# An attention and expert kernel: scores on 48 stacked rows in 64x64 tiles, and the step of a batch written out in eight slots

## The reference

```python
qkv = x @ w_qkv.T                       # 16 heads, D = 8
att = einsum('bhqd,bhkd->bhqk', q, k) / sqrt(8)
att = where((j <= i) & (j >= i - 127), att, -inf)   # window of 128
out = einsum('bhqk,bhkd->bhqd', softmax(att), v)
x = layernorm(x + out @ w_out.T)
logits = x @ router_w; p = softmax(logits); top 2 of 8
y = sum over the two of p_e * (gelu(x @ w_in[e] + b_in[e]) @ w_out[e] + b_out[e])
x = layernorm(x + y)
```

## Time and profile before

| what | value |
|---|---|
| median of 3 runs | 224.44 us (224.05 to 225.66) |
| the profiled execution's own time | 223.83 us |
| its span, first to last instruction | 221.8 us |
| PE busy | 203.4 us (92%) |
| DVE busy | 182.9 us (82%) |
| ACT busy | 116.7 us (53%) |
| POOL busy | 89.2 us (40%) |
| mean granted TensorE clock | 0.96 of full speed |

### The profile page before, as it was taken

One profiled execution on the slowest core, in us unless ns is written; L12 is line 12 of the kernel. 1 busy time (PEld: TensorE's weight loads), 2 busy tenths in 40 slices (PEclk: granted clock), 3 DMA queues, 4 the chain that ended last, 5 costly groups with the idle time before them and its releaser, 6 DMA issues.

```text
span 221.8 us, 5963 instructions
## 1 busy us (share of the span) xinstructions
PE 203.4 (92%) x1906; PEld 135.9 (61%) x1908; DVE 182.9 (82%) x522; ACT 116.7 (53%) x270; POOL 89.2 (40%) x166
## 2 busy tenths in 40 slices
PE   7786999989999999999999999989999899999960
PEld 4332446555565565565566566656688798989950
DVE  6664655789979989989989998977899888988883
ACT  2200106647557557557557566769445756374530
POOL 7230003375445635635635536478244211422103
PEclk9997559999999999999999999999999999999996
DMA  4947751542633533533533431000000001000011
GB/s 113 282 117 240 202 148 46 151 147 77 170 120 104 163 110 99 162 104 99 160 104 99 158 104 29 5 26 3 0 4 0 0 3 45 7 24 24 3 47 47
DMA packets 20391, 19.66 MB, mean 89 GB/s; under 512 B 1609, under 2 KB 17937, under 8 KB 20369
## 3 DMA queue, kind: packets, MB, share of 16 engines
q1 hardware_dynamic: 20180, 19.30, 29.4%
q10 hardware_dynamic: 189, 0.09, 0.1%
HBM read 13.94 MB, written 5.24 MB: 86 GB/s over the span
## 4 chain that ended last, share of the span: by engine, by line
PE 63%; DVE 17%; issue 7%; ACT 4%; DMA 4%; POOL 1%; SPq 1%; DVEq 1%; POOLq 0%; ACTq 0%
PE bank L1051 12%; PE bank L1043 9%; PE bank L960 7%; PE bank L977 5%; PE bank L992 4%; PE bank L955 3%; PE bank L942 3%; PE bank L945 3%; PE bank L926 3%; PE bank L1089 3%; DMA ks<-k_scratch 2%; DVE rest L671 2%; DVE neg_max L748 2%; PE bank L978 2%; DVE parts L676 2%
## 5 line engine op out<-in xcount | busy, mean ns | idle before, releaser
L474 ACT ACTIVATE probs<-bank 128x384 f32<-128x384 f32 x128 | 60.0, 496 | 34.7 <-PE bank L978 32.5
L432 POOL TENSOR_SCALAR_AFFINE_SELECT probs<-probs 128x1024 f32<-128x1024 f32 x32 | 35.7, 1116 | 67.8 <-ACT probs L474 67.8
L813 DVE SCALAR_TENSOR_TENSOR x_rows<-bank,gate_c,x_rows 128x128 f32<-128x128 f32 (+1 forms) x128 | 36.6, 343 | 5.3 <-PE bank L1051 4.2
L748 DVE TENSOR_REDUCE neg_max<-bank 128x2 f32<-128x384 f32 x64 | 33.5, 546 | 3.4 <-PE bank L960 3.1
L1051 PE MATMUL bank<-w_out_sb,hid 128*128 128x128 f32 x256 | 34.2, 277 | 1.0 <-DVE x_rows L813 1.0
L1051 PEld LDWEIGHTS bank<-w_out_sb,hid 128*128 128x128 f32 x256 | 32.6, 191 | 3.4 <-DVE x_rows L813 1.4
L574 ACT ACTIVATE hid<-bank,b_in_sb 128x512 f32<-128x512 f32 x32 | 21.9, 687 | 22.4 <-PE bank L1043 22.3
L977 PE MATMUL bank<-qs,ks 75*128 75x256 bf16 x128 | 33.4, 279 | 0.1
L743 DVE TENSOR_REDUCE neg_max<-bank 128x4 f32<-128x512 f32 x32 | 21.9, 685 | 8.8 <-PE bank L945 8.1
L978 PE MATMUL bank<-qs,ks 75*128 75x128 bf16 x128 | 26.9, 218 | 0.0
L436 POOL TENSOR_SCALAR_AFFINE_SELECT probs<-probs 128x512 f32<-128x512 f32 x32 | 24.2, 756 | 0.0
(11 more groups left out here) (117 smaller groups left out, 343.8 us busy)
## 6 DMA issues: line engine op xcount, KB each, us to landing
qs<-q_scratch SPq DMA_DIRECT2D x16, 288.0 KB
ks<-k_scratch SPq DMA_DIRECT2D x16, 288.0 KB
q_scratch<-parts SPq DMA_DIRECT2D x8, 192.0 KB, 2.1
k_scratch<-parts SPq DMA_DIRECT2D x8, 192.0 KB, 2.4
x_cols<-x_t SPq DMA_DIRECT2D x8, 128.0 KB, 2.6
x_rows<-x SPq DMA_DIRECT2D x8, 128.0 KB, 2.2
k_scratch<-parts SPq DMA_DIRECT2D x8, 128.0 KB, 2.3
out<-y_sb SPq DMA_DIRECT2D x8, 128.0 KB, 1.8
```

The source lines that it names most:

```text
L432: pool.affine_select(out=own, in_=own, compare_op=ALU.is_ge, fill=0.0, base=0, pattern=[[0, 2], [0, 4], [1, P]], channel_multiplier=-1).th ...
L474: nc.scalar.activation(probs[g][:, :, i, :], st_banks(spare)[k % len(st_banks(spare))][:, 0:3 * P].rearrange("p (k c) -> p k c", k=3), ACT ...
L748: nc.vector.tensor_reduce(neg_max[:, 1, 4 * g + 2 * u:4 * g + 2 * u + 2], score_bank[1 + u][:, 0:384].rearrange("p (h c) -> p h c", h=2), ...
L813: nc.vector.scalar_tensor_tensor(token_rows(c, n), y_bank[e % 4][:, n * E:(n + 1) * E], gate_of(c, n, e), token_rows(c, n), ALU.mult, ALU. ...
```

## The change

Only 6 of the 9 products of parts stay, so a head takes 48 rows. Two heads stand one above the other in the stacks, on partitions 0 to 47 and 64 to 111, and there are 8 pairs of heads a batch, each in one piece of a stack; four stack buffers take the place of two, and all a batch's rows come in one set of four transfers. In `scores` each matmul uses a tile of 64x64 of the array, so that four (two heads, two halves of the queries) stand side by side; for the first 128 queries each half now takes only the keys that it needs. The mask's matmuls are cut into the same tiles. `turned_scores` computes a pair of heads in two tiles of 64 rows by 128 columns, each into its own bank, and there is one such pair of banks in place of two alternating banks. One exponential takes both heads of a pair.

The split into parts changes hands: PE subtracts the top part inside the bank (`subtract_top`), ACT takes the middle part, DVE only the low one. The maxima are split in two operations a batch instead of eight.

The loop and the steps go. Every engine now walks 75 slots, eight for each batch: batch b's scores start in slot 8b (six of the eight slots have a job), its maxima are turned in 8b+8, its pairs of turned scores stand in slots 8b+11 to 8b+18, and its tail in 8b+22 to 8b+31; the projection for it stands in slot 8b-14. The first 11 slots have `keep_warm(2)` in place of turned scores. The loads of the later x columns (768 KB), the output weights and all rows of x are issued after the stacks of batches 0 and 1. The split of the expert weights and the choice for the first half of the tokens stand in slots 64 and 65 on DVE. The normed rows are written straight to their final tile, and POOL's copy of them goes. The last batch's transposed rows and logits move from chunk 0 of the experts into chunk 1, and the second half's choice stands later in chunk 1. The chunks are written out too.

```diff
-BLK = PARTS * D
-ROWS = PARTS * BLK
+PRODUCTS = ((0, 1), (0, 0), (0, 2), (1, 0), (1, 1), (2, 0))
+ROWS = len(PRODUCTS) * D
+KROWS = ROWS + PARTS
-KROWS = ROWS + PARTS
+PAIRS = H // 2
 QUADS = H // 4
...
-LOAD_WARM_UP = 7
-WARM_UP = 34
+LOAD_WARM_UP = 8
+WARM_UP = 44
...
+TWO_BF16_ONES = 1.0019378662109375
+STACKS = 4
+TURN_MAX, VALUES, S2, PV = 8, 12, 11, 15
+COPY_O, TURN_O, TURN_ATTN, PROJECT_OUT, TURN_X1, LOGITS = 22, 23, 25, 26, 30, 31
+PROJECT_QK = -14
+LAST_S1, LAST_S2 = 8 * B - 1, 8 * B - 1 + S2
+SCORE_JOBS = {0: (False, 0), 1: (True, 0), 2: (True, 2), 4: (False, 4), 5: (True, 4), 6: (True, 6)}
...
+                sp.wait_ge(part_top, b + 1)
+                copies(b, 0, 0)
+                copies(b, 1, 0)
+                sp.wait_ge(part_mid, b + 1)
+                copies(b, 0, 1)
+                copies(b, 1, 1)
+                sp.wait_ge(part_low, b + 1)
...
+            def stack(b):
+                sp.wait_ge(scratch_written[b % 2], 80 * (b // 2 + 1))
+                if b >= STACKS:
+                    sp.wait_ge(st_ready, PAIRS * (b - STACKS + 1))
+                for i, operand in enumerate((qs, ks)):
+                    for r in range(2):
+                        sp.dma_start(operand[b % STACKS][64 * r:64 * r + ROWS, :, :],
+                                     scratch[b % 2, i, :, r, :].rearrange("a (n t) -> a n t", n=PAIRS)).then_inc(stacked[b % STACKS], 16)
+            def stack_max(b):
+                sp.wait_ge(max_copied, b + 1)
+                for r in range(2):
+                    sp.dma_start(qs[b % STACKS][64 * r + ROWS:64 * r + KROWS, :, :],
+                                 max_t[r * PARTS * PAIRS:(r + 1) * PARTS * PAIRS, :]).then_inc(max_stacked[b % STACKS], 16)
...
+            write_parts(0)
+            sp.wait_ge(ones_ready, 1)
+            stack(0)
+            write_parts(1)
             sp.wait_ge(ones_ready, 2)
+            stack(1)
+            sp.dma_start(x_t_sb[:, 2 * T:B * T], x_t[:, 2 * T:B * T]).then_inc(x_t_loaded[2], 16)
+            sp.dma_start(wout_sb[:, :], wout_t).then_inc(out_w_loaded, 16)
+            sp.dma_start(router_sb[:, :], router_w).then_inc(moe_w_loaded, 16)
+            sp.dma_start(b_in_sb[:, :], b_in_t).then_inc(moe_w_loaded, 16)
+            sp.dma_start(x_sb[:, :, :], x.rearrange("(n p) e -> p n e", p=P)).then_inc(x_loaded, 16)
+            sp.wait_ge(ones_ready, STACKS)
+            for slot in range(LAST_S1 + 2):
+                b = batch_at(slot, TURN_MAX)
+                if b is not None:
+                    stack_max(b)
+                b = batch_at(slot, PROJECT_QK + 2)
+                if b is not None:
+                    write_parts(b)
+                b = batch_at(slot, PROJECT_QK + 3)
+                if b is not None:
+                    stack(b)
+                if slot == 9:
                     sp.dma_start(w_in_sb[:, :, :], w_in.rearrange("e d h -> d e h")).then_inc(moe_w_loaded, 16)
                     sp.dma_start(w_out_sb[:, :, :], w_out.rearrange("e h d -> h e d")).then_inc(moe_w_loaded, 16)
...
+            for slot in range(LAST_S2 + 2):
+                b = batch_at(slot, PROJECT_OUT + 1)
+                if b is not None:
+                    first_deviation(b)
+                n = quad_at(slot + PV - S2 - 2)
+                if n is not None:
+                    mask_probs(*n)
...
+            def exponentials(b, p):
+                g = p // 2
+                if p % 2 == 0 and b:
+                    act.wait_ge(pv_done, QUADS * (b - 1) + g + 1)
+                act.wait_ge(st_ready, PAIRS * b + p + 1)
+                two = slice(2 * (p % 2), 2 * (p % 2) + 2)
+                nc.scalar.activation(probs[g][:, :, two, :].rearrange("p k j c -> p j k c"),
+                                     st[:, :, 0:3 * P].rearrange("p j (k c) -> p j k c", k=3), ACT.Exp, scale=SCALE).then_inc(exp_done, 1)
...
+            def take_middle(b):
+                act.wait_ge(part_rest, b + 1)
+                nc.scalar.activation(parts[b % 2][:, 1, :, :], projection_bank(b)[:, :].rearrange("p (a t) -> p a t", a=2), ACT.Copy).then_inc(part_mid, 1)
...
+            for slot in range(LAST_S2 + 1):
+                n = pair_at(slot)
+                if n is not None:
+                    exponentials(*n)
+                for offset, piece in ((TURN_MAX, copy_max), (TURN_ATTN, copy_attention), (PROJECT_QK, take_top), (PROJECT_QK + 1, take_middle),
+                                      (VALUES, pad_v), (COPY_O, copy_output), (TURN_X1, copy_x1), (LOGITS, copy_logits)):
+                    b = batch_at(slot, offset)
+                    if b is not None:
+                        piece(b)
+                if slot == LAST_S1 + 2:
+                    route_exponentials(EARLY, 1)
...
+            def take_low(b):
+                p = parts[b % 2]
+                dve.wait_ge(part_mid, b + 1)
+                nc.vector.tensor_tensor(p[:, 2, :, :], projection_bank(b)[:, :].rearrange("p (a t) -> p a t", a=2), p[:, 1, :, :],
+                                        ALU.subtract).then_inc(part_low, 1)
...
+            def split_max(b):
+                part = max_parts[b % 2]
+                upper = upper_half(part[:, :, :, :, :])
+                dve.wait_ge(maxima, JOBS * (b + 1))
+                nc.vector.tensor_tensor(part[:, :, :, 1, :], part[:, :, :, 0, :], upper[:, :, :, 0, :], ALU.subtract).then_inc(max_rested, 1)
+                dve.wait_ge(max_rested, b + 1)
+                nc.vector.tensor_tensor(part[:, :, :, 2, :], part[:, :, :, 1, :], upper[:, :, :, 1, :], ALU.subtract).then_inc(max_split, 1)
...
+            for slot in range(LAST_S2 + 1):
+                b = batch_at(slot, TURN_O + 1)
+                if b is not None:
+                    normalise(b)
+                b = batch_at(slot, PROJECT_OUT + 1)
+                if b is not None:
+                    first_stats(b)
+                    first_moments(b)
+                b = batch_at(slot, TURN_X1 - 1)
+                if b is not None:
+                    first_norm(b)
+                n = jobs_at(slot)
+                if n is not None:
+                    take_maxima(*n)
+                b = batch_at(slot, TURN_MAX - 1)
+                if b is not None:
+                    split_max(b)
+                b = batch_at(slot, PROJECT_OUT)
+                if b is not None:
+                    first_residual(b)
+                b = batch_at(slot, PROJECT_QK + 1)
+                if b is not None:
+                    take_low(b)
+                b = batch_at(slot, TURN_X1 + 1)
+                if b is not None:
+                    split_x1(b)
+                if slot == LAST_S1 + 1:
+                    split_weights()
+                    route_shift(EARLY, B // 2 - 1)
+                if slot == LAST_S1 + 2:
+                    choose(EARLY, 1)
...
+            def subtract_top(b):
+                pe.wait_ge(part_top, b + 1)
+                mm(projection_bank(b)[:, :], minus_bf[:, :], parts[b % 2][:, 0, :, :], start=False, stop=True, skip_group_check=True).then_inc(part_rest, 1)
...
+            def scores(b, second, pair, job):
+                q, k = qs[b % STACKS], ks[b % STACKS]
+                heads, width = (2, 192) if second else (4, P)
+                if job % JOBS == 0:
+                    pe.wait_ge(stacked[b % STACKS], 64 * (b // STACKS + 1))
+                for r in range(2):
+                    if job + r >= 3:
+                        pe.wait_ge(maxima, job + r - 2)
+                    bank = score_bank[(job + r) % 3][:, 0:heads * width].rearrange("p (h c) -> p h c", h=heads)
+                    rows = slice(64 * r, 64 * r + 64)
...
+                        mm(at, ident_bf[rows, 64 * r:64 * r + 64], mask, start=True, stop=True)
+                for i in range(heads):
+                    for r in range(2):
+                        rows = slice(64 * r, 64 * r + ROWS)
+                        bank = score_bank[(job + r) % 3]
+                        for half in range(2):
+                            lo = 64 * half
+                            if second:
+                                keys, queries = slice(lo, lo + 192), slice(P + lo, P + lo + 64)
+                            else:
+                                keys, queries = slice(0, 64 + lo), slice(lo, lo + 64)
+                            last = mm(bank[lo:lo + 64, i * width:i * width + keys.stop - keys.start], q[rows, pair + i, queries], k[rows, pair + i, keys],
+                                      start=False, stop=True, skip_group_check=True)
+                        if i == heads - 1:
+                            last.then_inc(scores_ready, 1)
...
+            def turned_scores(b, p):
+                q, k = qs[b % STACKS], ks[b % STACKS]
+                if p == 0:
+                    pe.wait_ge(max_stacked[b % STACKS], 32 * (b // STACKS + 1))
+                if b or p:
+                    pe.wait_ge(exp_done, PAIRS * b + p)
+                for kt in range(2):
```

(48 more changed lines are left out.)

1100 lines of the change are left out of this document (417 added, 683 removed).

## The result

The changed kernel takes **229.91 us** (median of 8 executions, 226.93 to 232.35) against 225.22 before (8 executions, 223.85 to 225.66): 1.016 times as long, 95% interval 1.011 to 1.021. I had forecast 220 and faster: the time lies in the wide range of 209 to 231, outside the forecast's own of 214 to 226, and it moved the other way. The executions of the changed kernel spread over 5.4 us, those of before over 1.8, and they differ in the mean granted clock (0.892 to 0.916); the profiled one took 231.64, 1.7 above its median, with a span of 229.8.

A forecast was written before the change was run, and what follows sets the result against it. Steps bound by PE, DVE a microsecond behind. First exponential 44.5, slots 11 to 63 85.5 (to 130.0), first expert matmul 149.7, experts 60.4 (to 210.1), plus 7.3 and 2.0: 219.4, with 0.6 for the median 220 us; range 214 to 226, wide 209 to 231.

The forecast's parts named there:

- PE in a step: Scores and turned scores: two row halves overlap; PE saves 3.2 us a batch, giving 13.7 us a full batch.
- rivals 2 and 3: Row halves overlap partly (1.5 times one; 224; chance 0.12) or run in turn (3.4 us PE a batch; 239; 0.10).
- DVE and ACT in a step: Steps: DVE's sum falls 3.8 to about 11.5 us; ACT's exponential over two heads takes 0.8, middle part adds 0.6.
- The start gets longer: Slot 2 waits for late x columns, issued near 24.8; first exponential at 44.5 against 33.8, 10.7 us lost.
- The second queue: Start: batch 0's maxima rows queue on SP behind batch 2's parts and stack, landing at 44.
- Less the same 5.3 for light slots at both ends: Slots 11 to 63: 53 x 13.7 / 8 = 90.8, less 5.3 for lighter end slots, 85.5 us.
- I take them as just hidden, and a few tenths a batch if not: Maxima's rows in the steps: three slots, 5.1 us, for copy, two issues and landing.
- The clock: Experts: the colder clock after the standstill takes 1.5 us.
- Rival 4: Clock stays lower after standstills of 8, 2 and 7 us; about 9 us more, 229; chance 0.14.
- The end's chain: Slots 64 to 74: `weigh_values` in slot 69 waits behind choice, statistics and masking; first expert matmul at 149.7.
- The experts: Experts' part: 61.9 us as before, less 3 for earlier gates, plus 1.5 for colder clock: 60.4.
- Worth 3 at most: Experts: first-half gates ready well before the first shares, saving 3 us at most.

The follow-up runs named there:

- experiment 3: Changed kernel with the first half's choice of experts issued two operations a slot from slot 65 on instead of 16 in a row; 225.91 us.
- experiment 14: Changed kernel plus two matmuls of 512 idle columns a slot from slot 64 on, choice left in one piece; 230.24 us.
- 2: Changed kernel with the 1 MB of expert weights asked for in slot 22 instead of slot 9; 229.39 us.
- Experiment 12: Changed kernel with one edit: batch b's stack asked for behind the maxima's rows of batch b-2, in slot 8b-7; 226.47 us.
- experiment 11: Changed kernel plus idle PE matmuls ahead of three waits: 20 in slot 2, 8 each in slots 68 and 69; 225.64 us.
- experiment 13: Experiment 9's kernel plus two matmuls of 512 idle columns a slot from slot 64 on; 211.63 us.
- experiment 9: Changed kernel: batch 2's x columns earlier, x rows in slot 18, expert weights in slot 22, choice spread, maxima's rows on SP ahead of the stack; 215.98 us.
- experiment 5: Changed kernel with the two transfers of the maxima's rows issued by ACT behind its copy instead of by SP; 240.73 us.
- experiment 6: Changed kernel: batch 2's x columns earlier, expert weights in slot 22, choice spread, maxima's rows on ACT's queue, x rows in slot 18; 224.28 us.

## Why the prediction was wrong

For the profiled execution the forecast's sum gives 219.4, and it took 231.64, 12.2 more. That execution is 1.7 us above its median, and the sizes below are those of single executions:

| stretch | forecast | measured | difference |
|---|---|---|---|
| to the first exponential | 44.5 | 39.3 | -5.2 |
| slots 11 to 63 | 85.5 | 97.7 | +12.2 |
| slot 64 to the experts | 19.7 | 22.9 | +3.2 |
| experts to the end | 67.7 | 70.0 | +2.3 |
| outside the span | 2.0 | 1.8 | -0.2 |

- **PE in a step: right.** Two row halves run side by side. Timeline of PE: turned scores, masks, scores.

```profile
72.70 0.34 PE L936 MATMUL st<-qs,ks 51*128 51x256 bf16 x4
...
72.97 0.41 PE L910 MATMUL score_bank<-edges,ident_bf 64*64 64x512 bf16 x4
...
73.10 0.40 PE L921 MATMUL score_bank<-ks,qs 48*64 48x128 bf16 x16
...
73.43 0.49 PE L885 MATMUL misc<-wqkv_sb,x_t_sb 128*128 128x128 f32 x2
```

  From start to start a pair's turned scores take 0.27 us: 384 columns at 0.45 ns and 0.1 for the change of shape; in turn it would be 0.45. Masks and 16 score matmuls take 0.46, the 1024 columns' time that the forecast gave a first tile. A pair of row halves goes at two times one, and rivals 2 and 3 are out. By the estimate from the Trainium skill ("TensorE: Matmul & The Clock Gate", section "Why this matters for your kernels") two row tiles would have gone at 1.5 times one; the trace does not agree, with 0.27 us where that estimate makes 0.33 (1.33 times 0.17, and 0.1 for the change of shape).
- **DVE and ACT in a step: right** (11.6 and 10.7 against 11.5; an exponential over both heads 0.81 against 0.8).
- **"The start gets longer": right in place, too large in size.** The load was asked for at 19.68, not 24.8. The step that failed is SP's time table: batch 0's four stack issues ended at 12.1 and not near 16.5, and four such issues took 1.7 us (17.93 to 19.64) and not 3.5; against that the writes of batch 1 took 1.0 longer, landing by 17.9 instead of 21.3. The load itself took 6.5 us to let PE go, not 5.2. The second queue, batch 0's rows behind batch 2's stack, did not hold anything: SP had asked for the stack by 34.9, the rows were copied at 35.73 and asked for at 35.75, and PE waited 0.47 us for them. In the traces of 3, 14 and 2, whose start is the same, the first exponential came at 40.4, 41.5 and 42.1, so 39.3 is the earliest of four.
- **"Less the same 5.3 for light slots at both ends": wrong by 3.4 us.** With SP's order mended slots 11 to 63 took 90.1, and one batch in it was 1.2 above its like at the full clock (14.43 against 13.24): 88.9, not 85.5. The four batches from slot 27 on average 13.8 us at the full clock, not 13.7, which makes 0.9 of it; the other 2.5 are the light slots: the old kernel's light ends are not the new one's.
- **"I take them as just hidden, and a few tenths a batch if not" (the maxima's rows): wrong, 3.4 us in this execution.** It holds once the pipeline is level; batch 1's rows, copied at 46.90, stood behind batch 3's stack until 50.07. Experiment 12 shows it: 5.37 to 1.95. In experiment 3, with the order unchanged, it was 3.03, so up to 3.4 us and less in other executions.
- **The clock: the large failure, and the step that failed most.** The sum gave it 1.5 us, in the experts. It took 4.1 us in slots 19 to 23 (experiment 12), about 1.2 in another batch (15.43 us, against 14.25 for the same batch in experiment 12), and 3.2 in slots 64 to 74 (experiment 11), 8.5 together. Rival 4 had the mechanism, with a chance of 0.14. That its 229 lies so near 229.91 is in part luck: it put 9 us of low clock on top of the forecast's sum, and the other errors of that sum, +3.4, +3.4, +2.3 and -5.4, happen to leave 3.7 in a trace that is 1.7 above the median. The argument had the standstills in hand and took them as once-only costs; those of slots 2, 19 and 68 each brought their own stretch at the lower clock.
- **The end's chain: right in kind**, the wait for the choice and the masking included: with the clock mostly kept it took 19.6, and 19.7 was forecast. The forecast had one wait, in slot 69; the runs show two, and that the sum meets it to 0.1 is luck.
- **The experts: wrong by 2.7.** They took 63.1 us from the first matmul to the end of PE's last, against 60.4, and 6.8 behind it, not 7.3. "Worth 3 at most" was taken whole for the earlier gates, and it did not come: in experiment 13 the experts began at the full clock and still took 62.9 (139.75 to 202.61), where the kernel before took 61.9. The lower clock at their start then cost some tenths, not 1.5. What holds them I did not find.

The 3.4, 3.4 and 8.5 and the experts' 2.3 make 17.6, less 5.2 for the start and 0.2 outside: the 12.2. The edits of experiment 13 take 18.3 us off the changed kernel's time.

What stays open: the dips of some 3 us inside the steps (93.1 to 96.5 in the changed kernel, 79.3 to 82.7 even in the fastest), which come in another place in each kernel, in stretches where PE is recorded as busy. What sets how long the standstill of slot 19 gets in an execution, and how the clock's price divides in the executions without a trace, is open too.

## What to carry to other kernels

When work is taken off the bounding engine, price the clock with it: list every wait and every thin stretch that the change opens, and give each its own time at the lower clock, at what rows at that level show. Ask of every queue in order not only who is first behind a long issue, but who is behind it a batch later. Where a wait can't be removed, work that nobody reads may pay ahead of it, and where slots are thin but free of long waits, inside them; in the one trace that has filling inside the slots around a wait of 2 us (experiment 14), it did not hold the clock. Look at more than one execution before a stretch is given a price: slots 11 to 63 took 97.7 us in one and 90.6 in another with the same instructions up to there.

## What the runs showed of the hardware

- In the changed kernel the clock fell during waits of PE of 5.2 us (at 24.8) and 3.35 us (at 52.1) and was back at 31.7 and 65.8. It also fell without any wait above 1.5 us, in the thin slots of experiment 9 (0.50 from 130.6 to 147.7). With 0.5 us more PE work a slot it stayed at 1.00 (experiment 13).
- 24 KB took 7.5 us from the issue to their reader with a stack of 768 KB and 1 MB of weights asked for by another queue between 2.5 us before and 0.3 behind (experiment 5), 5.9 us with a stack asked for beside them and no weights (experiment 6), 3.4 us right behind a stack on SP's own queue (changed kernel, 50.07 to 53.45), and 3.1 us ahead of it (experiment 13, 28.80 to 31.88).
- Issuing two small transfers held ACT's queue for 1.5 to 2.1 us; moved there once a batch they made a full batch 0.7 us longer (14.97 and 14.28 in experiment 5, where the same batches took 14.25 and 13.55 without).
